# Own scores and maxima of a decoder-style attention as 128x128 tiles in PSUM, the maxima's rows moved by four transfers of SP, the own weight spread through memory, and value products in two runs per step

## The reference

```
q = (seq2 + b_self) @ Wq + bq                    # 8 x 512 x 512, 16 heads of 32
k = concat(x + b_prev, seq2 + b_self) @ Wk + bk
v = concat(x, seq2) @ Wv + bv
score_prev = q . k[first 512] * SCALE, masked where key >= seq_len
score_self = sum(q * k[own row]) * SCALE         # one score per query and head
w = softmax(concat(score_prev, score_self))
attn = w[:-1] @ v[first 512] + w[-1] * v[own row]
x = x + attn @ Wo + bo
h = gelu(x @ W1 + b1)                            # 2048 wide
x = x + concat(h @ W2 + b2, h @ We[expert] + be[expert])
```

## Time and profile before

| | us |
|---|---|
| median of 3 runs | 1902.25 (1897.83 to 1902.78) |
| profiled execution, own time | 1894.65 |
| its span | 1892.8 |
| PE busy | 1821.1 (96%) |
| DVE, ACT, POOL busy | 974.1, 755.3, 635.9 |

### The profile page before, as it was taken

The page is one execution under the profiler, slowest core; times in us unless marked ns, Lnnn a source line. Parts: engine busy times, 40 slices in busy tenths (PEclk is TensorE's granted clock), DMA queues, the critical chain, the costliest instruction groups (busy, mean ns, idle before and its releaser), DMA issues.

```text
span 1892.8 us, 27293 instructions
## 1 busy us (share of the span) xinstructions
PE 1821.1 (96%) x8288; PEld 1295.3 (68%) x8288; DVE 974.1 (51%) x1373; ACT 755.3 (40%) x1290; POOL 635.9 (34%) x492
## 2 busy tenths in 40 slices
PE   6999999999999999999997899999999999999997
PEld 5655656656566565565663578888888888888886
DVE  4577586776876768768667642313131313232311
ACT  3354454554544545445445342323232323323222
POOL 3277384765764847657556300000000000000000
PEclk8999999999999999999998699999999999999999
DMA  6262343432533325225314330303021213121111
GB/s 143 37 118 60 70 79 74 92 70 54 109 79 65 77 61 102 60 62 101 79 40 137 91 113 13 72 17 72 17 50 36 52 33 55 34 39 44 32 19 23
DMA packets 337244, 122.17 MB, mean 65 GB/s; under 512 B 285642, under 2 KB 304074, under 8 KB 337170
## 3 DMA queue, kind: packets, MB, share of 16 engines
q1 hardware_dynamic: 336658, 120.83, 29.7%
q10 hardware_dynamic: 512, 0.53, 0.1%
HBM read 53.63 MB, written 16.79 MB: 37 GB/s over the span
## 4 chain that ended last, share of the span: by engine, by line
PE 78%; DVE 8%; issue 4%; POOL 3%; SPq 2%; ACT 2%; DMA 2%; ACTq 1%; DVEq 0%; POOLq 0%
PE ps_proj L1117 13%; PE ps_av L1069 6%; PE ps_av L1070 6%; PE ps_av L1071 6%; PE ps_max L1147 5%; PE ps_score L1181 5%; PE ps_av L1194 5%; PE ps_proj L1069 3%; PE ps_max L1070 3%; PE ps_score L1070 3%; PE ps_score L1069 3%; PE ps_max L1069 3%; PE ps_max L1071 3%; PE ps_score L1071 3%; PE ps_proj L1070 3%
## 5 line engine op out<-in xcount | busy, mean ns | idle before, releaser
L634 ACT ACTIVATE p_f<-ps_score 128x512 f32<-128x512 f32 x512 | 303.9, 598 | 441.3 <-PE ps_score L1181 366.4
L840 DVE TENSOR_REDUCE m_col<-ps_max 128x1 f32<-128x512 f32 x512 | 331.6, 684 | 219.1 <-PE ps_max L1147 218.5
L518 POOL TENSOR_TENSOR p_sum<-p_sum,p_f 128x512 f32<-128x512 f32 x256 | 346.1, 1365 | 95.5 <-ACT p_f L634 94.0
L1002 DVE TENSOR_TENSOR h_lo<-h_f,h_hi 128x512 fp32r<-128x512 f32 x128 | 88.3, 690 | 480.9 <-ACT h_hi L731 480.7
L515 POOL TENSOR_TENSOR p_sum<-p_f 128x512 f32<-128x512 f32 x128 | 162.7, 1296 | 267.9 <-PE ps_av L1203 260.2
L1181 PE MATMUL ps_score<-stacks 99*128 99x512 f32 x512 | 223.1, 438 | 9.6 <-ACT p_f L634 8.8
L1117 PE MATMUL ps_proj<-in_hi,w_hi 128*128 128x512 f32 x512 | 206.8, 404 | 10.5 <-POOL in_lo L523 6.7
L1117 PE MATMUL ps_proj<-in_hi,w_lo 128*128 128x512 f32 x512 | 205.0, 400 | 0.0
L1117 PE MATMUL ps_proj<-in_lo,w_hi 128*128 128x512 f32 x512 | 204.3, 399 | 0.0
L1147 PE MATMUL ps_max<-stacks 97*128 97x512 f32 x512 | 180.3, 412 | 21.7 <-DVE m_col L840 13.4
L1069 PE MATMUL ps_av<-y_hi,w_hi 128*128 128x512 f32 x512 | 199.5, 390 | 1.6 <-DVE y_lo L998 1.6
(11 more groups left out here) (129 smaller groups left out, 2863.8 us busy)
## 6 DMA issues: line engine op xcount, KB each, us to landing
stacks<-parts SPq DMA_DIRECT2D x384, 128.0 KB
raw<-in_x_dram SPq DMA_DIRECT2D x128, 64.0 KB, 2.0
raw<-in_fside_BxSxS_dram SPq DMA_DIRECT2D x128, 64.0 KB, 2.2
attn_scratch<-num SPq DMA_DIRECT2D x32, 256.0 KB, 2.3
x_raw<-in_x_dram SPq DMA_DIRECT2D x128, 64.0 KB, 2.1
a_raw<-attn_scratch SPq DMA_DIRECT2D x32, 256.0 KB, 3.3
we_raw<-in_L_cond_We_dram SPq DMA_DIRECT2D x32, 256.0 KB, 2.7
out_dram<-z_t SPq DMA_DIRECT2D x128, 64.0 KB, 1.9
```

The source lines that it names most:

```text
L518: pool.tensor_tensor(p_sum[:, j], p_sum[:, j], now, ALU.add).then_inc(sum_made, 1)
L634: act.activation(p_f[:, i % FLIGHT], ps_score[i % 2][:, :], ACT.Exp, scale=SCALE).then_inc(p_made, 1)
L840: dve.tensor_reduce(m_col[:, n % C, n // C:n // C + 1], ps_max[n % 2][:, :], AX.X, ALU.max).then_inc(max_made, 1)
```

## The change

Own scores and maxima become 128x128 tiles: query block t at partitions 32t, head j (and again at j + 4 for the maxima) inside it, 128 queries along. Their products go to four 32-column strips. ACT doubles the columns of the maxima first. DVE takes the maximum into free columns of PSUM (`m_s`), makes the negated high part and, for the second four rows, the low part, and subtracts the maximum from the own scores. SP, not ACT, moves the maxima's rows: four transfers, one per block of queries, at the start of its list for the step, ahead of the stacks (and, in step 1, ahead of loads 4 to 7). The weight of the own score is taken on 128x128, stored to memory by ACT, and read back by SP with four transfers that copy each row to 32 partitions, behind the stacks. The products with `sum_spread` and `spread` are gone, and so are qk's high and low parts. Value products go in two runs of eight (i=1: t=2 and 3 of the step before; i=9: t=0 and 1), with the denominators, own scores and turned maxima behind the second; at i=1 they stand behind the projections now. `p_f` has 16 buffers. POOL's sums are six later in its list, DVE's denominator goes to i=11, the reciprocals to 13 and 14, normalize to 15.

```diff
-    FLIGHT = 2 * HG
+    FLIGHT = 4 * HG
 # SP
+            def maxima(b, c):
+                G, r = C * b + c, c % 2
+                sp.wait_ge(m_lo_made, G + 1)
+                for t in range(C):
+                    sp.dma_start(f(q_st[KM:KM + 2, r, :, P * t:P * (t + 1)]),
+                                 f(m_neg[DH * t:DH * t + 2 * HG, :])).then_inc(m_landed[r], DMA)
+            def own_weights(b, c):
+                G, r = C * b + c, c % 2
+                sp.wait_ge(ow_stored, DMA * (G + 1))
+                wait(sp, attn_made, G - 1)
+                for j in range(HG):
+                    sp.dma_start(den[DH * j:DH * (j + 1), r].rearrange("d (t q) -> d t q", q=P),
+                                 own_dram[r, :, j].partition_broadcast(DH)).then_inc(ow_landed[r], DMA)
...
                     if g == 1 and not last:
                         for j in range(C):
                             load(b + 1, j)
+                    if last and g == 2:
+                        for n in range(6):
+                            wide(n)
+                    if not (last and g == C - 1):
+                        maxima(*after(b, g, 1))
                     if more:
                         for j in range(HG):
                             if g == 1 and j % 2 == 0 and not last:
                                 load(b + 1, C + j)
                                 load(b + 1, C + j + 1)
                             stack(*after(b, g, 2), j)
                     if last and g == 2:
-                        for n in range(10):
+                        for n in range(6, 10):
                             wide(n)
+                    if not (last and g == C - 1):
+                        own_weights(*after(b, g, 1))
 # POOL
-                        if i == 3:
+                        if i == 8:
                             own_value(b, g)
-                        if i >= HG:
-                            add_probabilities(b, g, i // HG, i % HG)
+                        n = (i + 6) % TILES
+                        if i >= 10:
+                            add_probabilities(b, g, 1 + n // HG, n % HG)
+                        elif n < SUMS and not (first and g == 0):
+                            add_probabilities(*after(b, g, -1), 1 + n // HG, n % HG)
 # ACT
+            def maxima_twice(b, c):
+                act.wait_ge(max_made, TILES * (G + 1))
+                act.copy(m_col[:, :, HG:2 * HG], m_col[:, :, 0:HG]).then_inc(m_twice, 1)
...
-                act.copy(m_row[:, :], ps_max[1][0:HG, :]).then_inc(own_made, 1)
+                act.copy(own_s[:, :], ps_max[1][:, 0:P]).then_inc(own_made, 1)
...
-                act.activation(den[:, c % 2], ps_max[1][:, :], ACT.Exp, scale=SCALE).then_inc(ow_made, 1)
+                act.activation(own_s[:, :], own_s[:, :], ACT.Exp, scale=SCALE).then_inc(ow_made, 1)
...
+                act.dma_start(own_dram[c % 2].rearrange("t k q -> (t k) q"), own_s[:, :]).then_inc(ow_stored, DMA)
...
-                if t < 2:
-                    wait(act, sum_made, sums_of(C * b + g - 1, t + 2, j))
-                else:
-                    act.wait_ge(sum_made, sums_of(C * b + g, 1, j))
+                wait(act, sum_made, sums_of(C * b + g - 1, max(t, 1), j))
 # DVE, at i == 10
+                dve.tensor_tensor(m_s, ps_max[0][:, 0:P], own_s[:, :], ALU.max).then_inc(m_s_made, 1)
+                dve.tensor_scalar(m_hi[:, :], m_s, -1.0, None, ALU.mult).then_inc(m_hi_made, 1)
+                dve.scalar_tensor_tensor(out=m_neg[:, :], in0=f(m_hi[:, :]), scalar=less_hi[:, 0:1], in1=m_s,
+                                         op0=ALU.mult, op1=ALU.subtract).then_inc(m_lo_made, 1)
+                dve.tensor_tensor(own_s[:, :], own_s[:, :], m_s, ALU.subtract).then_inc(own_less_made, 1)
 # PE
+                for t in range(C):
+                    mm = pe.matmul(ps_max[1][DH * t:DH * (t + 1), 0:P], sum_heads[:, :], qk_f[:, P * t:P * (t + 1)],
+                                   start=True, stop=True)
...
+                    mm = pe.matmul(ps_max[0][DH * t:DH * t + 2 * HG, 0:P], m_col[:, t, :], f(ident[:, :]),
+                                   start=True, stop=True)
...
-                        if i == 1 and not (first and g == 0):
-                            value_burst(*after(b, g, -1), C - 1)
-                        if i > 1 and i % HG == 1:
-                            value_burst(b, g, i // HG - 1)
-                        if i == HG + 1 and not (first and g == 0):
-                            denominators(*after(b, g, -1))
...
+                        if i == 1 and not (first and g == 0):
+                            for t in (2, 3):
+                                value_burst(*after(b, g, -1), t)
+                        if i == 9:
+                            for t in (0, 1):
+                                value_burst(b, g, t)
+                            if not (first and g == 0):
+                                denominators(*after(b, g, -1))
-                        if bound and i == 10:
+                        if bound and i == 9:
                             own_scores(*nxt)
                             turn_max(*nxt)
-                        if bound and i == 13:
-                            own_less_max(*nxt)
```

More of the change, by code:

```diff
@@ L377, in _ @@
                 stack(0, 1, j)
+            maxima(0, 0)
+            own_weights(0, 0)
             for dst, src in ((bv_col[:, :], bv), (bo_col[:, :], bo), (bias_1[:, :], b1), (bias_2[:, 0:CS], b2)):
@@ L695, in batch @@
                             q_out(*nxt2)
-                        if i == 11 and maximum:
-                            m_high(*nxt)
-                        if i == 12 and maximum:
-                            maxima(*nxt)
                         if last:
@@ L841, in maximum, with own_max @@
                                   ALU.max).then_inc(max_made, 1)
-            def max_row(b, c):
+            def own_max(b, c):
                 G = C * b + c
@@ L847, in max_row, with m_parts, own_less_max @@
                 dve.wait_ge(turn_mm, G + 1)
-                dve.tensor_tensor(m_row[:, :], ps_max[0][0:HG, :], m_row[:, :], ALU.max).then_inc(m_row_made, 1)
-            def m_low(b, c):
-                dve.wait_ge(m_hi_made, C * b + c + 1)
-                dve.scalar_tensor_tensor(out=m_neg[QUAD:QUAD + HG, :], in0=m_row[:, :], scalar=-1.0,
-                                         in1=f(m_neg[0:HG, :]), op0=ALU.mult, op1=ALU.subtract).then_inc(m_lo_made, 1)
+                dve.tensor_tensor(m_s, ps_max[0][:, 0:P], own_s[:, :], ALU.max).then_inc(m_s_made, 1)
+            def m_parts(b, c):
+                G = C * b + c
+                dve.wait_ge(m_s_made, G + 1)
+                dve.tensor_scalar(m_hi[:, :], m_s, -1.0, None, ALU.mult).then_inc(m_hi_made, 1)
+                pb, pc = after(b, c, -1)
+                wait(dve, m_landed[pc % 2], C * DMA * (2 * pb + pc // 2 + 1))
+                dve.wait_ge(m_hi_made, G + 1)
+                dve.scalar_tensor_tensor(out=m_neg[:, :], in0=f(m_hi[:, :]), scalar=less_hi[:, 0:1], in1=m_s,
+                                         op0=ALU.mult, op1=ALU.subtract).then_inc(m_lo_made, 1)
+            def own_less_max(b, c):
+                dve.wait_ge(m_s_made, C * b + c + 1)
+                dve.tensor_tensor(own_s[:, :], own_s[:, :], m_s, ALU.subtract).then_inc(own_less_made, 1)
             def numerator(b, g):
@@ L920, in _ @@
             weights_low(2, 2)
-            qk_low(0, 0)
             for t in range(3 * C):
@@ L929, in _ @@
             qk(0, 1)
-            max_row(0, 0)
-            m_low(0, 0)
+            own_max(0, 0)
+            m_parts(0, 0)
+            own_less_max(0, 0)
             def batch(b, first, last):
@@ L942, in batch @@
                                 maximum(*nxt, n)
-                        if i == 5 and bound:
-                            qk_low(*nxt)
                         if i == 3 and started:
                             numerator(*after(b, g, -1))
-                        if i == 7 and started:
+                        if i == 11 and started:
                             denominator(*after(b, g, -1))
@@ L953, in batch @@
                             k_low(*nxt2)
-                        if i == 11 and bound:
-                            max_row(*nxt)
+                        if i == 10 and bound:
+                            own_max(*nxt)
                         if i == q_at[g] + 1 and project:
                             q_low(*nxt2)
-                        if i == 11 and bound:
-                            m_low(*nxt)
-                        if i in (10, 13) and started:
-                            for n in range(2) if i == 10 else range(2, 4):
+                        if i == 10 and bound:
+                            m_parts(*nxt)
+                            own_less_max(*nxt)
+                        if i in (13, 14) and started:
+                            for n in range(2) if i == 13 else range(2, 4):
```

(1 more changed line is left out.)

124 lines of the change are left out of this document (45 added, 79 removed).

## The result

Median 1958.26 us (1950.64 to 1966.0, 4 runs) against 1901.41 (1897.83 to 1902.78) for the kernel before, which ran beside it: 1.0307 times, 95% interval 1.0288 to 1.0326. The forecast was 1896.8, range 1860 to 1922: wrong in sign and size. The profiled execution took 1959.29, its span is 1957.5, 64.7 longer than before.

A forecast was written before the change was run, and what follows sets the result against it. PE, busy for 96% of the span, was taken as the bound, with POOL setting step g=2. Gains of 40.0 us less 34.5 given back made -5.5 net; with the median 7.6 above the profiled run, 1896.8 us, range 1860 to 1922.

The forecast's parts named there:

- the second wait of step g=2: In g=2, stack 0 queues behind maxima and loads 4 and 5; its 5.2 us were taken as hidden under POOL's chain.
- PE's gain (2.3): PE's saving per step from products dropped and joined runs, less sixteen narrow products: 2.3 us (1.4 to 2.9).
- The wait charged at the start of a step: After the turned maxima, PE waits mainly for the stack: 1.15 us in g=0, 0.6 in g=1, 0.85 in g=3.
- rival B: SP's eight new issues per step bound every step; gain gone from 0.25 us more, 1919 us at 1.0; chance 0.20.
- Clock: PE stays as busy as before in the steps, so I price none: PE's granted clock in the steps was taken as unchanged, so no time was charged for it.
- Step g=2 (+4.0: POOL's later order delays the next batch's first query product: period 33.4 us against 29.4, so +4.0 per step.
- The count of 19 instructions: POOL's 8 low parts and 11 sums up to in_low 7, at 1.31 us each, take 24.9 us.
- Under this wait, and costing nothing more, lies another: Sentence on g=2: stack 0's lateness, 5.2 us, lies under POOL's wait and would show only if POOL were faster.
- POOL, not PE, sets that step: Reading of the earlier trace in g=2: the next batch's first query product starts at 517.55, as POOL's in_low ends at 517.49.
- End (+6.5: After the last turned maxima, the final sums start later behind denominators moved to i=9: +6.5 us (3 to 11).
- Prologue: Prologue and first step save own scores, own-less-max and lead-in: -2.0 us.
- The last batch's g=2: Without loads or projections, DVE bounds it; qk_low, a denominator and PE's runs leave its way: -2.7 us.

The follow-up runs named there:

- 10: The tiles alone, with own_value behind the last sum, loads 4 and 5 ahead of the maxima, and low parts 0 to 3 early: 1895.43 us.
- 6: The changed kernel with loads 4 and 5 ahead of the maxima and turns, high and low parts 0 to 3 at i=6 to 9 of step 1: 1912.26 us.
- 9: The kernel of 6 with, in steps 1 and 3, stack 0 ahead of the maxima and ACT issuing their blocks 2 and 3: 1888.4 us.
- 11: The kernel of 10 with, in steps 1 and 3, stack 0 ahead of the maxima and ACT issuing their blocks 2 and 3: 1874.2 us.
- experiment 2: The changed kernel with SP issuing loads 4 and 5 ahead of the maxima in step 1, nothing else: 1957.42 us.
- 7: The changed kernel with turns, high and low parts 0 to 3 at i=6 to 9 of step 1, loads still behind the maxima: 1951.9 us.
- the tiles alone: The changed kernel with value products in four runs, POOL's and DVE's order and 8 p_f buffers as before, own_value still at i=8: 1999.37 us.
- experiment 5: The tiles alone, with POOL's own_value moved from i=8 to behind the last sum of a step: 1913.47 us.

## Why the prediction was wrong

Four steps of it failed: the stack lands 1.0 to 1.65 us later than it had it; the clock was priced at nothing; the second wait of step g=2 was said to cost nothing more; and no term had DVE held by POOL.

**PE's gain (2.3): right in kind.** By the rows 2.8, by busy time 1.9 to 2.9. It decided nothing.

**The wait charged at the start of a step: too small, because the stack lands later.** PE was ready for it nearly when the forecast had it, at T+6.6, 7.5 and 8.4 in the periods ending in g=0, 1 and 3 (forecast 6.3, 7.3, 8.1). The stack landed at T+9.1, 8.4 and 9.9 (forecast 7.45, 7.3, 8.9). So PE waited for it 2.5, 1.0 and 1.6 us, where 1.15, 0.6 and 0.85 were charged. In g=0 the 1.65 us of lateness has three parts: SP is free at T+4.1, not T+3.3 (a transfer of the maxima is 0.67, not 0.55, and m_neg is ready at T+1.3, not T+1.1); the stack is issued 0.35 later still; and it lands 4.7 behind its issue, not 4.15. The first part was rival B, which named 0.25 us as the point where the gain is gone. In that it was right, but its own price, 22 steps of 0.77, is 17 us, of the 61 by which the forecast missed.

Joining the runs took 1.0 us of PE's work (the run at i=13) away from between T and the stack. The forecast's times for PE had that in them, so it is no error of the sum. But it is a cost of the change: with separate runs (10) the step ending in g=3 is 26.9, with joined ones (6) 28.8.

**"Clock: PE stays as busy as before in the steps, so I price none": the term that was put at nothing.** The clock fell all the same. From the windows of the changed kernel ending in g=0: the same 185 instructions are 34.7 busy at 1.00, 36.3 at 0.96, 37.4 at 0.91, so the lower level costs 1.6 to 2.7 us there. PE's new idle time goes with it. Where PE waits 3.9 to 4.6 us for the stack (all seven steps ending in g=2) the clock of the window is 0.75 to 0.86, where it waits 2.0 to 2.7 (g=0) it is 0.91 to 0.96 in five windows and 1.00 in two, and with that wait taken away (9 and 11) it is 1.00 in all seven. What exactly makes it fall is open: two waits of 2.5 us left it at 1.00, and in experiment 2 it is 0.81 to 0.85 in steps ending in g=2 in which no single wait reaches 2 us.

**Step g=2 (+4.0, measured +7.3).** The count of 19 instructions was right: with the stack's wait gone (2), in_low 7 ends at T+26.2 to 27.0, and T+26.6 was forecast. The sentence that failed is "Under this wait, and costing nothing more, lies another". Through exponential and high part it makes in_low 7 0.9 to 2.0 us later in the five regular steps. From in_low 7 to the next T it is then 7.3 to 8.1 us, not 6.8, partly at the lower clock; experiment 2 has that too, without the long wait. Two more steps are 4.5 us longer by the hold told of below. Experiments 2, 6 and 7 show the two limits of nearly equal height. The rest of that passage came out: with POOL's chain shorter (7) PE stands 5.6 to 6.4 us for the stack, where it said 5.2. Also the reading of the earlier trace rows, "POOL, not PE, sets that step", is not borne out for the kernel before. Two rows that touch show who is last in order; POOL had waited 1.94 us for PE's denominators one instruction earlier.

**What no step had: the hold of DVE by POOL.** POOL starts its sums late, with all p in place, and in the changed kernel it works from 519.78 to 535.87, for 16 us, without a pause. From the period of 40.17 us (DVE, then POOL):

```profile
529.30 7.11 DVE L901 TENSOR_TENSOR num<-num,den 128x512 f32<-128x512 f32 x1
...
533.35 2.52 POOL L537 TENSOR_TENSOR p_sum<-p_sum,p_f 128x512 f32<-128x512 f32 x2
```

The normalize ends 0.54 behind POOL (535.87), and PE's next max tile waits 3.34 for DVE. It happened in two of the seven steps ending in g=2 (40.2 and 40.9 us); the other 30 normalizes take 1.8 us at most.

**The edges.** End (+6.5, measured +9.2): right in kind, too small; the runs of values at half clock take 3.6 each there, as assumed. Prologue: right in sign (-2.0, measured -1.0). The last batch's g=2 (-2.7, measured +1.2) has the wrong sign: PE is idle there for 3.1 us, before 3.3, and busy 1.4 longer, at a clock of 0.82, before 0.96. That is the clock term again.

**How the 84 us between the changed kernel and the best one divide,** taken in this order: loads first and low parts early 46, stack 0 first with split maxima 24, separate runs with the order of POOL and DVE that goes with them 14 (experiments 6, 9 and 11). With separate runs already in place the queue's order gave 21. Of the first 46 the loads alone gave 1 (2) and the low parts alone 6 (7). How much of the 46 is the hold of DVE was not tried apart.

## What to carry to other kernels

When work leaves the busiest engine, list what it covered: whatever used to land behind it may now be waited for, and idle time in one piece can cost again in clock. Queue order on the engines with slack was worth more here than the change itself (one POOL instruction behind the sums instead of ahead of them took 86 us off the tiles alone, experiment 5): an instruction that may wait belongs behind those that can't be late. Before calling a wait hidden, follow what it delays; if it feeds the chain that hides it, it is not.

## What the runs showed of the hardware

A DVE operation that reads two operands in SBUF, 0.7 us by itself, can take 7.1 to 9.3 us while POOL runs sums without a gap. In the three places shown it ends 0.54 to 0.56 us behind the start of POOL's pause, even of a pause of 0.27. The Trainium skill (SBUF — State Buffer, section "SBUF: two separate sides") says that such an operation and one of POOL exclude each other for the whole instruction, whichever starts first. The traces agree in so far as the DVE operation in these places gets through only at POOL's pause; by that rule the wait would be one POOL instruction, 1.3 us, and here it was five or more. It is not always so: at 457.42 in the changed kernel a normalize took 1.54 in the midst of eight of POOL's sums. What decides between the two is open.

Narrow products in four column strips run at 0.034 us per instruction (16 in 0.55) in a window with a clock of 1.00. A transfer of eight rows of 128 columns takes SP 0.67 us to issue, more than the 0.63 of a stack's (1.88 for three) and far more than the 0.26 of a mask.
